# Output projection in fp16 parts, one ScalarE copy placed earlier, router bias as a full-height product

## What is computed

```python
def _L1_attn_ref(hidden_states, wq, wk, wv, wo):
    ...
    out = jnp.einsum('bhqk,bhkd->bhqd', attn, v)
    out = out.transpose(0, 2, 1, 3).reshape(b, s, N_HEADS * HEAD_DIM)
    return out @ wo.T
def _L1_ffn_ref(x, A, B, Wr, br):
    router_logits = jnp.einsum('bsd,hd->bsh', x, Wr) + br
    scores = H * jax.nn.softmax(router_logits, axis=-1)
    low = jnp.einsum('bsd,hrd->bshr', x, A)
    out = jnp.einsum('bshr,hor,bsh->bso', low, B, scores)
    return SCALING * out
...
x = x + _layernorm(_L1_attn_ref(_layernorm(x, axis=-1), L1_attn_wq, ...), axis=-1)
x = x + _layernorm(_L1_ffn_ref(_layernorm(x, axis=-1), L1_ffn_A, L1_ffn_B, L1_ffn_Wr, L1_ffn_br), axis=-1)
```

## Time and profile before

| | us |
|---|---|
| runs: median of 3 (lowest, highest) | 1484.44 (1482.44, 1486.02) |
| the profiled execution | 1490.9 |
| its span | 1489.0 |
| TensorE busy in the span | 1292.4 (87%) |
| last stage, from its first instruction to the end of the span | 1349.59 to 1489.0 |

### The profile page before, as it was taken

How to read it: one execution, slowest core, us unless ns; L and a number is a source line. 1 busy time by engine, 2 the same in 40 slices (tenths; PEclk the granted TensorE clock), 3 DMA queues, 4 the chain that set the end, 5 groups by cost and what they waited for, 6 DMA issues and landing times. The chain is left out here.

```text
span 1489.0 us, 34856 instructions
## 1 busy us (share of the span) xinstructions
PE 1292.4 (87%) x10654; PEld 706.9 (47%) x10750; DVE 1021.5 (69%) x3215; ACT 873.5 (59%) x1605; POOL 449.2 (30%) x1388
## 2 busy tenths in 40 slices
PE   8957999999996996699899898998988989986995
PEld 3423444444443553355455455554555545543653
DVE  5875656556563599588788787887878878852563
ACT  2524625444250565377787687786767867872553
POOL 3530000000002233233334333433434334331665
PEclk9975999999998998599999999999999999998997
DMA  9310000000000266301110011110111101002221
GB/s 325 158 43 0 1 1 0 0 0 0 0 1 3 71 164 164 131 26 40 41 39 32 11 39 41 39 39 8 36 41 39 39 7 39 9 9 57 57 79 43
DMA packets 65131, 69.73 MB, mean 47 GB/s; under 512 B 35214, under 2 KB 53774, under 8 KB 64300
## 3 DMA queue, kind: packets, MB, share of 16 engines
q1 hardware_dynamic: 64940, 67.38, 14.2%
HBM read 36.96 MB, written 19.92 MB: 38 GB/s over the span
## 5 line engine op out<-in xcount | busy, mean ns | idle before, releaser
L1305 ACT ACTIVATE arena<-bank 128x512 f32<-128x512 f32 x576 | 340.2, 612 | 171.4 <-PE bank L1225 97.8
L1365 DVE TENSOR_REDUCE arena<-bank 128x32 f32<-128x512 f32 x528 | 343.8, 683 | 104.3 <-PE bank L1211 65.7
L1211 PE MATMUL bank<-arena 96*128 96x512 bf16 (+3 forms) x832 | 235.7, 333 | 25.2 <-issue 20.6
L1225 PE MATMUL bank<-arena 123*128 123x512 bf16 x576 | 222.8, 396 | 14.9 <-ACT arena L1305 12.3
L1244 PE MATMUL bank<-arena 128*32 128x128 f32 x4608 | 176.3, 276 | 12.6 <-ACT arena L1305 12.4
L579 PE MATMUL bank<-arena 128*128 128x512 f16 (+1 forms) x704 | 173.3, 390 | 0.0
L1475 POOL TENSOR_SCALAR arena<-arena 128x128 bf16<-128x128 bf16 x384 | 142.6, 371 | 47.5 <-DVE arena L1425 25.5
L1244 PEld LDWEIGHTS bank<-arena 128*32 128x32 f32 x4608 | 124.8, 109 | 43.2 <-ACT arena L1305 23.8
L1463 POOL TENSOR_TENSOR arena<-arena 128x4 f32<-128x4 f32 x128 | 25.4, 199 | 373.0 <-DVEq L1400 343.1
L205 POOL TENSOR_TENSOR arena<-arena 128x1 f32<-128x1 f32 x32 | 7.5, 234 | 388.8 <-DVE arena L201 388.4
L591 PE MATMUL bank<-arena 128*128 128x512 f16 (+1 forms) x528 | 118.4, 386 | 3.1 <-ACT arena L651 3.1
(11 more groups left out here) (183 smaller groups left out, 2252.6 us busy)
## 6 DMA issues: line engine op xcount, KB each, us to landing
arena<-qk_rows SPq DMA_DIRECT2D x16, 960.0 KB, 4.8
qk_rows<-arena SPq DMA_DIRECT2D x16, 768.0 KB, 4.1
arena<-arena SPq DMA_DIRECT2D x32, 256.0 KB, 2.9
arena<-in_x SPq DMA_DIRECT2D x4, 1024.0 KB, 12.4
out<-arena SPq DMA_DIRECT2D x16, 256.0 KB, 2.1
qk_rows<-arena SPq DMA_DIRECT2D x16, 192.0 KB, 4.6
arena<-in_down_qT SPq DMA_DIRECT2D x1, 2816.0 KB, 25.6
arena<-in_up_qT SPq DMA_DIRECT2D x1, 2752.0 KB, 19.4
```

Of the source, the lines that this page charges most:

```text
L1211: last = pe.matmul(bank[:, at:at + k1 - k0], query_aug[st.slot][0:ROWS, h * P:(h + 1) * P], key_aug[st.p][0:ROWS, k0:k1], start=True, stop ...
L1225: last = pe.matmul(bank[:, :], key_aug[st.p][0:KROWS, j * P:(j + 1) * P], query_aug[st.slot][0:KROWS, f * N:(f + 1) * N], start=True, stop ...
L1305: act.activation(probs[u % PROBS], back_bank[u % 2][:, :], ACT.Exp, scale=float(HD) ** -0.5).then_inc(probs_ready, 1)
L1365: dve.tensor_reduce(out=cm[:, number * per:(number + 1) * per], in_=score_bank[bank_of_score(front, number)][:, :].rearrange("p (c d) -> p ...
```

## The change

The output projection no longer multiplies in fp32. At the end of `attention`, GpSimd scales woT by 64 and splits it into two fp16 parts, high and rest. ScalarE's `keep_o` now writes turned o as fp16 (`o_high`); a new VectorE step, `keep_o_rest`, subtracts that from the bank and writes the remainder as fp16 (`o_rest`). `feed_o` makes three passes of four fp16 products, high by high, high by rest, rest by high. The scale of 64 is undone by the layer normalisation, with an eps of its own. ScalarE runs `keep_ls` ahead of normalising x. The bias is a product over all 128 rows, of which only the first is not zero.

```diff
@@ attention, GpSimd, after its last unit
+            wo, wo_high, wo_rest = output_weights(m)
+            pool.wait_ge(m.last_in, 16 * LAST_LOADS)
+            pool_seq.mark(pool.tensor_scalar(out=wo, in0=wo, scalar1=WO_UNIT, scalar2=None, op0=ALU.mult))
+            pool_seq.wait(pool)
+            pool_seq.mark(pool.tensor_copy(wo_high, wo))
+            pool_seq.wait(pool)
+            pool.tensor_tensor(out=wo_rest, in0=wo, in1=wo_high, op=ALU.subtract).then_inc(wo_parted, 1)
+            pool.wait_ge(wo_parted, 1)
@@ output_and_routed, TensorE
                 pe.wait_ge(gathered[k % 2], k // 2 * 16 + 16)
                 if k >= 1:
-                    pe.wait_ge(oT_ready, k)
+                    pe.wait_ge(o_rest_ready, k)
...
-                pe.wait_ge(oT_ready, k + 1)
+                pe.wait_ge(o_high_ready, k + 1)
                 if k >= 2:
                     pe.wait_ge(normal_ready["y"], k - 1)
-                for dc in range(DC):
-                    last = pe.matmul(y_bank[k % 2][:, :], oT[k % 2][:, dc * P:(dc + 1) * P], woT[:, dc * D:(dc + 1) * D],
-                                     start=dc == 0, stop=dc == DC - 1)
+                for n, (o, w) in enumerate(((o_high, wo_high), (o_high, wo_rest), (o_rest, wo_high))):
+                    if n == 2:
+                        pe.wait_ge(o_rest_ready, k + 1)
+                    for dc in range(DC):
+                        last = pe.matmul(y_bank[k % 2][:, :], o[k % 2][:, dc * P:(dc + 1) * P], w[:, dc * D:(dc + 1) * D],
+                                         start=n == 0 and dc == 0, stop=n == 2 and dc == DC - 1)
...
-                pe.matmul(bank[:, LR:LOW_N], ones, m.f32(BR_AT, LORA_H)[0:1, :], start=False, stop=True).then_inc(low_made, 1)
+                pe.matmul(bank[:, LR:LOW_N], ones, br_rows, start=False, stop=True).then_inc(low_made, 1)
@@ ScalarE
-                act.activation(oT[k % 2], o_bank[:, :], ACT.Copy).then_inc(oT_ready, 1)
+                act.activation(o_high[k % 2], o_bank[:, :], ACT.Copy).then_inc(o_high_ready, 1)
...
+                if holds(k - LAG_LS):
+                    keep_ls(k - LAG_LS)
                 if holds(k - LAG_NORMED):
                     normal("x", k - LAG_NORMED, xn, m.x(k - LAG_NORMED))
-                if holds(k - LAG_LS):
-                    keep_ls(k - LAG_LS)
@@ VectorE
+            def keep_o_rest(k):
+                dve.wait_ge(o_high_ready, k + 1)
+                if k >= 2:
+                    dve.wait_ge(made["y"], k - 1)
+                dve.tensor_tensor(out=o_rest[k % 2], in0=o_bank[:, :], in1=o_high[k % 2], op=ALU.subtract).then_inc(o_rest_ready, 1)
...
                 if holds(k - LAG_X):
                     add_y(k - LAG_X)
+                if holds(k + 1):
+                    keep_o_rest(k + 1)
                 if holds(k):
                     dve.wait_ge(made["y"], k + 1)
                     statistics("y", k, y_bank[k % 2][:, :])
@@ GpSimd, start of the stage
-            pool.memset(ones, 1.0).then_inc(ones_ready, 1)
+            pool_seq.mark(pool.memset(eps_y, EPS * WO_UNIT ** 2))
+            pool_seq.mark(pool.memset(br_rows, 0.0))
+            pool_seq.mark(pool.memset(ones, 0.0))
+            pool_seq.wait(pool)
+            pool.wait_ge(m.last_in, 16 * LAST_LOADS)
+            pool.tensor_copy(br_rows[0:1, :], m.f32(BR_AT, LORA_H)[0:1, :]).then_inc(ones_ready, 1)
+            pool.memset(ones[0:1, :], 1.0).then_inc(ones_ready, 1)
```

More of the change, by code:

```diff
@@ L991, in attention @@
     take = m.taker(CWORK, WOT_AT)
-    spare = m.taker(LWORK, ARENA - SEQ)
+    spare = m.taker(LWORK, WO_PARTS_AT)
     N = GQ * P
@@ L1027, in attention @@
     w_blank, top_ready, own_ready, diag_ready = s("d_w_blank"), s("d_top"), s("d_own"), s("d_diag")
+    wo_parted = s("d_wo_parted")
     dve_seq, pool_seq = Count(s("d_dve_seq")), Count(s("d_pool_seq"))
@@ L1500, with output_weights @@
 LWORK = BR_AT + 16
+WO_PARTS_AT = ARENA - SEQ - DC * D
+WO_UNIT = 64.0
+def output_weights(m):
+    n = DC * D
+    return m.f32(WOT_AT, n), m.f16(WO_PARTS_AT, n), m.f16(WO_PARTS_AT + n // 2, n)
 def output_and_routed(nc, m, s, dram):
-    woT, low_w = m.f32(WOT_AT, DC * D), m.f32(LOWW_AT, DC * LOW_N)
+    (_, wo_high, wo_rest), low_w = output_weights(m), m.f32(LOWW_AT, DC * LOW_N)
     LR = LORA_H * LORA_R
-    take = m.taker(LWORK, ARENA)
+    take = m.taker(LWORK, WO_PARTS_AT)
     two = lambda n: [take(n) for _ in range(2)]
-    o_tile, oT, yn = two(D), two(D), two(D)
+    o_tile, yn = two(D), two(D)
+    o_high, o_rest = ([take(D, F16) for _ in range(2)] for _ in range(2))
+    eps_y = take(1)
     xn, xT, zn = two(D), two(D), two(D)
@@ L1512, in output_and_routed @@
     peak, total, share = two(1), two(1), two(1)
-    ones = take(P)[0:1, :]
+    ones, br_rows = take(P), take(LORA_H)
     stats, mv, var, mean, rstd, shift = ({c: two(n) for c in "yxz"} for n in (6, 2, 1, 1, 1, 1))
@@ L1516, in output_and_routed @@
     o_bank, x_bank, y_bank, low_bank, ls_bank, z_bank = m.banks[0], m.banks[1], m.banks[2:4], m.banks[4:6], m.banks[6], m.banks[7]
-    gathered, o_turned, oT_ready = [s(f"e_gathered{b}") for b in range(2)], s("e_o_turned"), s("e_oT")
+    gathered, o_turned = [s(f"e_gathered{b}") for b in range(2)], s("e_o_turned")
+    o_high_ready, o_rest_ready = s("e_o_high"), s("e_o_rest")
     made = {c: s(f"e_made_{c}") for c in "yz"}
@@ L1605, in _ @@
             pe.wait_ge(m.last_in, 16 * LAST_LOADS)
-            pe.wait_ge(ones_ready, 1)
+            pe.wait_ge(ones_ready, 2)
             turn_o(0)
@@ L1686, in shares @@
                                   in1=score[p].unsqueeze(2).to_broadcast([P, LORA_H, LORA_R]), op=ALU.mult).then_inc(ls_ready, 1)
+            keep_o_rest(0)
             for k in rounds():
@@ L1709, in root @@
                 pool.wait_ge(stats_ready[c], k + 1)
-                pool_seq.mark(pool.tensor_tensor(out=var[c][p], in0=mv[c][p][:, 1:2], in1=m.eps[:, 0:1], op=ALU.add))
+                pool_seq.mark(pool.tensor_tensor(out=var[c][p], in0=mv[c][p][:, 1:2], in1=eps_y if c == "y" else m.eps[:, 0:1], op=ALU.add))
                 pool_seq.wait(pool)
```

## The result

| | before | changed |
|---|---|---|
| median of the runs (lowest, highest), us | 1485.23 (1482.44, 1487.06), 4 runs | 1472.38 (1468.12, 1473.86), 4 runs |
| profiled execution, its span | 1490.9, 1489.0 | 1468.12, 1466.3 |
| last stage, first gather to the end of the span | 139.4 | 122.1 |

The ratio is 0.991, with a 95% interval of 0.9884 to 0.9937: 12.9 us faster. The forecast was 1469 (1465 to 1476), so the time is inside the range and 3.4 us over the forecast.

The account below looks back on a forecast made before the run. Tied limits, TensorE's work at 6.72 us a round and a ring through `keep_ls` at 6.76, bound the last stage. Fill −2.0, eleven rounds −10.0 and drain −3.6 sum to −15.6: 1484.44 to 1469 us, range 1465 to 1476.

Parts of the forecast that it names:

- Two tied limits: Last stage's rounds: TensorE's work 6.72 us; ring from z's statistics through x's normalisation, `keep_ls` and `feed_z` 6.76; freeing one gives nothing.
- Three fp16 passes, 0.216 each: `feed_o`: twelve fp16 products at 0.216 us take 2.59 against 3.44, −0.85 us a round.
- rival D: `feed_o`: each fp16 pass costs its listed 390 ns; slower, 1502 us, deciding from 0.30 us a pass; 3%.
- C: Steady rounds stay at 6.7 us because something unseen holds the ring; only the drain is won, 1481 us; 3%.
- The bias, −0.06 a round: TensorE's bias product at 128 rows: 0.30 us against 0.36, −0.06 a round, ends −0.04 and −0.10.
- 0.7 us of slack in front of `turn_x`: Steady rounds: normalising x ends after 5.6 us, `turn_x` comes at 6.3, so 0.7 us is left.
- rival A: Steady rounds: the slack before `turn_x` is eaten, a second ring paces them at 6.0 to 6.5, 1471 to 1476 us; 15%.
- Subtraction and split: VectorE's subtraction, 0.69 us (0.42 to 1.2), is covered; GpSimd's weight split, 9.1 to 11.3 us, fits its idle time, costing nothing.
- The fill, −2.0: Start of the last stage, to the start of `feed_o(4)`: −2.0 us in all, including +0.65 for `turn_o(1)` awaiting the subtraction.
- Rival B: Fill: TensorE's gap before normalised x brings the clock down, costing 1.5 to 3 us, 1471 to 1472; 8%.
- The drain, −3.6: Stage's end: last `feed_o` with bias −0.9, `feed_z` waits for `keep_ls` −0.4 and −2.3, together −3.6 us.
- Its own signs: `feed_o` 5.8 to 5.9 apart, passes 0.216, no drain `feed_z` wait for `keep_ls`, span end near 1473, weights before 1341.

Follow-up runs that it names:

- the run with two passes: Change with the store a round later and shares without the scaling operation, now also without the pass of o's high part by the weights' rest: 1462.72 us.
- the pair of runs without other limits: Change with the store a round later and shares without the scaling operation: 1467.45 us; the same with the bias again as a 1-row product: 1470.38 us.

## Why the prediction was right, and where it was not

- **Two tied limits, and the order as the key.** Right. 6.72 for TensorE's own work (the order alone) and 6.76 to 6.77 for the ring (without the order) are the forecast's numbers.
- **Three fp16 passes, 0.216 each.** Right: twelve by starts in 2.59. Wherever the granted clock is 1.00, the fp16 passes of `feed_o` start 0.215 to 0.217 apart in all the profiles that have them, so neither a faster pass nor rival D's of 0.30 or more was seen there; at a clock of 0.50 they start 0.43 apart. C (rounds stay at 6.7) is what happens without the order, and with it doesn't.
- **The bias, −0.06 a round.** The mis-sized term. Both bounds, −0.04 and −0.10, came from fp32 rows as if the product of 8 columns cost what one of 136 does, and they left the passes of `low` alone. Measured with the waiting apart: 0.31 to 0.14 for itself and 1.02 to 0.93 for `low`, so −0.26 on top of the 0.04 of waiting. With this the round on TensorE is 5.58, not 5.85.
- **0.7 us of slack in front of `turn_x` (rival A).** The missed step. The forecast summed VectorE's and GpSimd's durations from before along y's way, and one of them is not constant: the scaling of the shares goes from 0.23 to 0.96 when it falls on `add_z`. With that a ring closes which the forecast did not have, through VectorE and GpSimd alone, at 5.78 to 5.80; the wait at `turn_x` is what it leaves TensorE. Rival A had a pace of 6.0 to 6.5, and 5.8 is below the forecast's own 5.85. Two misses that nearly cancel, then: 0.27 too much for the bias's round, 0.2 too little for the wait. That the eleven rounds came to −10.3 and −9.8 against −10.0 is luck, and no proof of the steps.
- **The gather behind the store.** Not in the forecast at all. At 6.72 and 6.77 a round, landings of 4.1 to 4.3 us were hidden (the order alone, the change without the order); at 5.6 one of 4.4 costs 1.2 to 1.4 us in the change, and there were one and two such rounds in its two profiles.
- **Subtraction and split.** Right. The subtraction takes 0.675 on average, where 0.69 was taken, and is covered. GpSimd's group of three:

```profile
1324.13 5.37 POOL L1487 TENSOR_SCALAR arena<-arena 128x2048 f32<-128x2048 f32 x1
...
1329.58 1.89 POOL L1489 CAST arena<-arena 128x2048 f16<-128x2048 f32 x1
...
1331.55 4.08 POOL L1491 TENSOR_TENSOR arena<-arena 128x2048 f16<-128x2048 f32 x1
...
1344.23 0.10 POOL L1754 MEMSET arena<- 128x1 f32 x1 [8.60 <-POOLq L1140]
```

  11.5 us from first start to last end, just above the bound of 11.3 (the scaling is 5.37 where it was held to be between 2.3 and 4.5), with 8.6 us to spare.
- **The fill, −2.0.** −1.3 and +0.1 measured in the two profiles. Rival B happened: held at 8%, it shows in every profile taken of the fp16 output without the extra products, and cost 2.0 us, inside its price of 1.5 to 3. The clock of 0.50 at the stage's start accounts for the difference between the two: it ended 10.6 us after the first gather in before, 8.9 in the first profile, 10.7 in the second. With like set against like, the fill gained nothing. The row of 2.75 us idle at full clock (granted 1.00) was taken as reassurance. But in before `feed_o(1)` of 3.6 us and a set of transposes (0.6) stood right ahead of that gap, and 3.8 us passed between one `feed_o` and the next. In the change the gap follows `feed_o(1)` of 2.75 at once, and 5.1 us pass.
- **The drain, −3.6.** −5.8 and −3.6 measured. Of the waits of 0.41 and 2.40, 0.38 and 0.61 are still there, so they did not go as forecast. What the first profile gained beyond −3.6 goes with the clock: three of before's last `feed_z` ran at a clock of 0.50 for all or most of their length (2.08, 2.01, 2.07), and only one did there, but three did in the second. The order alone, with one slow `feed_z`, gives 5.2 (28.0 against 33.2).
- **Its own signs.** Two of five came plainly: passes 0.216 apart, and the weights done before 1341 (1335.6). `feed_o` was not 5.8 to 5.9 apart in most rounds, `feed_z` still waited for `keep_ls` in the drain, and the span ended at 1466.3 and 1474.9, to both sides of 1473. Its sign against itself, a clock that falls again after 1361 and before the drain, came in the second profile to the letter (0.50 from 1366.4 to 1373.2), and in the first from 1359.9 to 1366.7.
- **The total.** The stage of the first profile is 17.4 shorter, that of the second 13.4, and the medians of the two sets of runs differ by 12.9 and 15.2. The forecast's −15.6 lies between the two stages, within both intervals and above both medians. The time is in the range largely because a bias term taken too small made up for the ring, the late gathers and the clock in the fill. Without the ring and the waits for gathers the stage takes 120.5, without the low stretch in the fill too 117.6, against 122.1 and 126.0.

What stays open: why the clock stays at 1.00 in before's fill, with 2.75 us idle, and falls to 0.50 in the change's, with 2.60; and whether the instruction packets make the gathers late, or only come with what does.

## What to carry to other kernels

When two limits are tied, as TensorE's work at 6.72 and a ring at 6.76 here, price the edits as a set: without the order the faster products and the bias gave nothing, the bias alone nothing, and the order alone 0.3%. (The faster products by themselves were not run.) Before shortening a round, list everything that was hidden by its old length (a DMA's tail, an operation on one engine that may fall on one of another, a ring through the other engines), since each becomes a limit in turn, here at 5.80, 5.58 and 5.42. A product of full height can be cheaper than one of a single row (here 0.14 us against 0.31). A short idle gap can cost again behind it, here 2.0 us after 2.60. And one profile of a change is one execution: the same kernel's drain took 27.4 us in one and 29.5 in the other.

## What the runs showed of the hardware

- **A small VectorE operation held by a large one on GpSimd.** The scaling of 128x8 takes 0.23 alone and up to 1.09 when GpSimd's `add_z` runs; in each of the long cases of the change's two profiles it ends 0.03 us after `add_z`. With a PSUM bank as its first operand, the operation in its place takes 0.35 with or without `add_z`; in the run with two passes it starts and ends inside it (1405.82 to 1406.17). The two differ in the operation, in its shape (128x128 against 128x8) and in the bank operand; which of these keeps it clear of `add_z` no run shows.
- **A one-row product among full-height ones** takes 0.31 for two passes of 8 columns and adds 0.09 to the eight passes ahead of it; with 128 rows, 127 of them zero, it takes 0.14, and those eight passes 0.93 instead of 1.02. That is 0.29 a round in the pair of runs without other limits.
- **A gather of 256 KB inside SBUF** lands 2.9 us after its issue as a rule, and after 4.05 to 4.54 in the 21 of 196 cases in which a 16 KB packet of the instruction queue starts 0.4 to 2.4 us behind the issue.
- **The granted clock** fell from 1.00 to 0.50 in the gap of 2.60 us in the fill, and stayed at 1.00 when ten products stood in that gap. With six products before the first gather landed it was still 0.50 until 10.2 us after that gather, and the first `feed_o` took 4.44.
